# ScalarE's two passes over a slot change places, and the weights get a semaphore of their own

## The reference, cut to what matters

```python
h = _L0_tok_ref(x, ...)
h = h + _L0_attn_ref(_layernorm(h, axis=-1), ...)
h = h + _L0_ffn_ref(_layernorm(h, axis=-1), ...)
```

```python
scores, idx = jax.lax.top_k(sim, PK_TOPK)
final_scores, pk_idx = jax.lax.top_k(score, FINAL_TOPK)
final_scores = jax.nn.softmax(final_scores, axis=-1)
k = jnp.einsum('bnhk,bnhkd->bnhd', kv_scores, keys_table[ind])
v = jnp.einsum('bnhk,bnhkd->bnhd', kv_scores, values_table[ind])
```

## Time and profile before

| | before |
|---|---|
| median of 3 runs | 11975.05 us (11971.79 to 11983.34) |
| the profiled execution's own time | 11981.82 us |
| its span, first to last instruction | 11980.0 us |
| PE busy | 11034.8 us (92%) |
| DVE busy | 10219.1 us (85%) |
| POOL busy | 8419.7 us (70%) |
| ACT busy | 7851.7 us (66%) |
| mean granted clock of TensorE | 0.981 |

### The profile page before, as it was taken

The page is one execution under the profiler, slowest core; times in us unless marked ns, Lnnn a source line. Parts: engine busy times, 40 slices in busy tenths (PEclk is TensorE's granted clock), DMA queues, the critical chain, the costliest instruction groups (busy, mean ns, idle before and its releaser), DMA issues.

```text
span 11980.0 us, 263894 instructions
## 1 busy us (share of the span) xinstructions
PE 11034.8 (92%) x70396; PEld 9154.4 (76%) x70396; DVE 10219.1 (85%) x42192; ACT 7851.7 (66%) x17926; POOL 8419.7 (70%) x8196
## 2 busy tenths in 40 slices
PE   3999999999999999999999999999999999999999
PEld 2777777777777777777777777777777777777777
DVE  6889888888888898888888988888889888888883
ACT  2666666666666666666666666666666666666665
POOL 0677777677777777777777777767777777777776
PEclk6999999999999999999999999999999999999999
DMA  2566566565565665665655656656556566566554
GB/s 66 155 173 179 156 174 171 160 175 167 166 177 159 171 179 157 171 172 161 175 166 164 177 158 170 179 155 174 170 161 177 165 168 177 158 172 177 158 170 137
DMA packets 1651836, 1975.58 MB, mean 165 GB/s; under 512 B 336238, under 2 KB 1125870, under 8 KB 1649902
## 3 DMA queue, kind: packets, MB, share of 16 engines
q1 hardware_dynamic: 1387950, 1418.48, 40.8%
q0 software_dynamic: 262144, 537.40, 17.2%
HBM read 1881.20 MB, written 73.40 MB: 163 GB/s over the span
## 4 chain that ended last, share of the span: by engine, by line
PE 57%; DVE 19%; ACT 8%; issue 7%; DMA 6%; SPq 2%; POOL 0%; DVEq 0%; ACTq 0%; POOLq 0%
PE bank L1008 16%; PE bank L1044 10%; PE bank L1031 6%; PE bank L1018 5%; DVE decay L1579 4%; PE bank L891 4%; ACT bank L1255 4%; DMA moving<-keyspace 3%; DVE apart L1709 3%; DMA wide<-states 3%; DVE onehot L1804 2%; PE bank L995 2%; PE bank L972 2%; DVE decay L1588 2%; PE bank L1060 2%
## 5 line engine op out<-in xcount | busy, mean ns | idle before, releaser
L819 POOL DMA_INDIRECT gath<-in_table_dram,rowsT x8192 | 8419.5, 1028 | 3533.0 <-issue 2449.9
L1262 ACT ACTIVATE weight<-bank 128x512 f32<-128x512 f32 x4096 | 2441.0, 596 | 2895.2 <-PE bank L1018 2863.6
L1008 PE MATMUL bank<-weight,rowtab 128*128 128x256 f32 x16384 | 4263.0, 382 | 0.0
L1008 PEld LDWEIGHTS bank<-weight,rowtab 128*128 128x128 f32 x16384 | 3122.9, 191 | 756.2 <-issue 20.6
L1255 ACT ACTIVATE bank<-bank,seventeen 128x512 f32<-128x512 f32 x4096 | 2711.5, 662 | 14.7 <-PE bank L1018 11.5
L1044 PEld LDWEIGHTS bank<-spread,gath 128*128 128x128 f32 x16384 | 2160.3, 192 | 149.6 <-issue 14.5
L1044 PE MATMUL bank<-spread,gath 128*128 128x96 f32 x16384 | 2116.5, 272 | 5.5 <-DMA gath<-in_table_dram,rowsT 5.1
L1031 PE MATMUL bank<-moving,pick_b 96*128 96x512 bf16 x4096 | 1584.5, 387 | 485.1 <-ACT bank L1255 392.4
L1018 PE MATMUL bank<-moving,pick_b 96*128 96x512 bf16 x4096 | 1562.2, 381 | 81.3 <-DMA moving<-keyspace 80.7
L1579 DVE TENSOR_TENSOR_SCAN decay<-decay,wide 128x256 f32<-128x256 f32 x2048 | 1238.4, 670 | 3.3
L1031 PEld LDWEIGHTS bank<-moving,pick_b 96*128 96x128 bf16 x4096 | 438.1, 107 | 924.6 <-ACT bank L1255 738.3
(11 more groups left out here) (268 smaller groups left out, 16949.8 us busy)
## 6 DMA issues: line engine op xcount, KB each, us to landing
rowtab<-in_tableD_dram SPq DMA_DIRECT2D x2048, 256.0 KB
wide<-states SPq DMA_DIRECT2D x512, 512.0 KB
moving<-keyspace SPq DMA_DIRECT2D x4096, 64.0 KB
gath<-in_table_dram,rowsT POOLq DMA_INDIRECT x8192
moving<-keyspace SPq DMA_DIRECT2D x4096, 32.0 KB
pix<-in_x_dram SPq DMA_DIRECT2D x504, 256.0 KB
keyspace<-split SPq DMA_DIRECT2D x256, 256.0 KB
out_dram<-acc SPq DMA_DIRECT2D x64, 64.0 KB
```

Of the source, the lines that this page charges most:

```text
L819: pool.indirect_dma_start(out=gath[:, u % RING, j, :], out_offset=None, in_=table, in_offset=bass.IndirectOffsetOnAxis(ap=rowsT[k][:, col: ...
L1008: mm(dense_ps[:, 0:TOK], rowtab[:, r, s % 2 * 2 + half, :], weight[s % 2][:, half * TOK:(half + 1) * TOK], start=(s % 16 == 0 and half == ...
L1262: ins = af(weight[s % 2][:], zd_ps[s % 2][:], ACT.Exp, scale=-1.0)
```

## The change

ACT does l(n) ahead of w(n-1) in every row of its table. Items that stood between the two stand behind both now; the order of all other items is kept. Every w signals a new semaphore, `weight_ready`; before, w signalled nothing but in the last slot of all. PE's `o` and `d` wait for `weight_ready` where they waited for `over_ready`; `z` still waits for `over_ready`. PE's own order stays.

```diff
-2 w1+0 S.hi3+0 l2+0 F.g+1 F.sq0+2
+2 l2+0 w1+0 S.hi3+0 F.g+1 F.sq0+2
...
-8 w7+0 F.kv2+2 l8+0
+8 l8+0 w7+0 F.kv2+2
...
-24 w23+0 F.sc+2 l24+0
+24 l24+0 w23+0 F.sc+2
...
+        weight_ready = sem("weight_ready")
...
-                    pe.wait_ge(over_ready, b * SLOTS + s + 2)
+                    pe.wait_ge(weight_ready, b * SLOTS + s + 1)
...
-                wait(pe, over_ready, b * SLOTS + s)
+                wait(pe, weight_ready, b * SLOTS + s - 1)
...
-                    pe.wait_ge(over_ready, IMAGES * SLOTS + (0 if s == 0 else 1))
+                    pe.wait_ge(weight_ready, IMAGES * SLOTS - (1 if s == 0 else 0))
...
-                ins = af(weight[s % 2][:], zd_ps[s % 2][:], ACT.Exp, scale=-1.0)
-                if isinstance(b, int) and b == IMAGES - 1 and s == SLOTS - 1:
-                    ins.then_inc(over_ready, 1)
+                af(weight[s % 2][:], zd_ps[s % 2][:], ACT.Exp, scale=-1.0).then_inc(weight_ready, 1)
```

More of the change, by code:

```diff
@@ L143 @@
 ACT_ORDER = """
-0 w63-1 l0+0 k3-1 a5.5-1 F.sq2+2 F.sq3+2 S.E2+0
-1 w0+0 l1+0 K3-1
-2 w1+0 S.hi3+0 l2+0 F.g+1 F.sq0+2
[L147 to L151, removed]
-8 w7+0 F.kv2+2 l8+0
[L153 to L167, removed]
-24 w23+0 F.sc+2 l24+0
[L169 to L207, removed]
+0 l0+0 w63-1 k3-1 a5.5-1 F.sq2+2 F.sq3+2 S.E2+0
+1 l1+0 w0+0 K3-1
+2 l2+0 w1+0 S.hi3+0 F.g+1 F.sq0+2
+3 l3+0 w2+0 a6.0-1
+4 l4+0 w3+0 F.sq1+2
+5 l5+0 w4+0 S.n+1 S.mi3+0
+6 l6+0 w5+0 a6.4-1 F.kv0+2
+7 l7+0 w6+0 S.E3+0 F.kv1+2 a6.5-1
+8 l8+0 w7+0 F.kv2+2
+9 l9+0 w8+0 F.kv3+2 S.tb+1 S.s0+1
+10 l10+0 w9+0 F.kv4+2 F.kv5+2
+11 l11+0 w10+0 F.kv6+2 F.kv7+2 S.s1+1 a7.0-1
+12 l12+0 w11+0
+13 l13+0 w12+0 F.kv8+2 S.s2+1 F.kv9+2
@@ new lines @@
+14 l14+0 w13+0
+15 l15+0 w14+0 a7.4-1 F.kv10+2 F.kv11+2
+16 l16+0 w15+0 a7.5-1 F.rs0+2 k0+0
+17 l17+0 w16+0 K0+0
+18 l18+0 w17+0 F.t0+2 S.s3+1 a0.0+0
+19 l19+0 w18+0
+20 l20+0 w19+0
+21 l21+0 w20+0 a0.4+0
+22 l22+0 w21+0
+23 l23+0 w22+0
+24 l24+0 w23+0 F.sc+2
+25 l25+0 w24+0 a0.5+0
+26 l26+0 w25+0
+27 l27+0 w26+0 a1.0+0
+28 l28+0 w27+0
+29 l29+0 w28+0 F.t1+2
+30 l30+0 w29+0 a1.4+0
+31 l31+0 w30+0 F.rs1+2
+32 l32+0 w31+0 k1+0 a1.5+0 K1+0
+33 l33+0 w32+0 S.wd+1
+34 l34+0 w33+0 F.t2+2 S.ln+1 F.ez+2
@@ new lines @@
+35 l35+0 w34+0 S.hi0+1 a2.0+0
+36 l36+0 w35+0 F.sg+2
+37 l37+0 w36+0
+38 l38+0 w37+0 S.mi0+1 S.hi1+1 a2.4+0
+39 l39+0 w38+0 S.cp+1 F.dt0+2
+40 l40+0 w39+0 F.xd+2 F.dt1+2
+41 l41+0 w40+0 a2.5+0 F.dc0+2
+42 l42+0 w41+0 S.E0+1 S.mi1+1
+43 l43+0 w42+0 a3.0+0
+44 l44+0 w43+0 F.dc1+2
+45 l45+0 w44+0 F.dc2+2
+46 l46+0 w45+0 a3.4+0
+47 l47+0 w46+0 F.dc3+2
+48 l48+0 w47+0 k2+0 F.dc4+2 a3.5+0 K2+0
+49 l49+0 w48+0
+50 l50+0 w49+0 F.dc5+2 S.E1+1
+51 l51+0 w50+0 a4.0+0
+52 l52+0 w51+0 S.wg+1
+53 l53+0 w52+0 F.dc6+2
@@ L208 @@
+54 l54+0 w53+0 F.dc7+2
+55 l55+0 w54+0 a4.4+0
+56 l56+0 w55+0 a4.5+0
+57 l57+0 w56+0
+58 l58+0 w57+0 S.hi2+1
+59 l59+0 w58+0 a5.0+0
+60 l60+0 w59+0
+61 l61+0 w60+0
+62 l62+0 w61+0 a5.4+0
+63 l63+0 w62+0 S.mi2+1
 """
```

## The result

The changed kernel takes **12014.01 us** (median of 6 runs, 12000.78 to 12027.21) against 11974.92 (6 runs, 11970.24 to 11983.34) for the kernel before on the same chip. The ratio is **1.0034 [1.0024, 1.0044]**: 0.34% slower, some 41 us. The forecast was 3 us faster. The time lies in its range, and it is that of its second rival (12011 to 12038).

What follows compares the result with a forecast made beforehand. Bound by a PE chain through l in a period's first half, then DVE with transfers or a mixture in alternate periods. 2 x 0.34 - 0.57 = 0.11 us per pair, some 31 pairs: 3 us off 11975, 11972; range 11905 to 12035.

Steps and rivals of the forecast that it cites:

- second rival: Items held back on ACT reach PE late in rows 8, 15, 55: 36 or 63 us slower, 12011 to 12038; chance 0.21.
- The count of a slot: Bare slots on PE: z starts 0.50 us earlier, but next o waits for w, at 1.69 instead of 1.90; gain 0.21.
- The four items without cover: ACT items made 0.57 later in rows 8, 15, 25, 55 cost PE 0.43, 0.57, 0.12 and 0.57 us.
- z's waits: PE's idle time ahead of z for l would shrink from 392 us to under 100.
- DVE's idle time ahead of acc: DVE's waits ahead of L1838 would hardly change.
- what DVE lets through in the first half: Up to row 39, DVE's nearly gapless stretch passes on only 0.34 us a period of PE's gain.
- every gap as used to the full: DVE's idle gaps of 0.15, 0.47 and 0.21 us after 4928.91 turn 0.49 late into 0.34 early by row 39.
- lies beside DVE's work: Row 55's 0.57 us loss is hidden in one of two periods and on the path in the other.
- if row 55 turned up in the chain of every period: Sign that the prediction is wrong: row 55 in the chain that ended last in all periods.
- earlier z changes nothing: Second half of the period whose chain is DVE's own with transfers: no gain there, the first half's is carried on.
- The likeliest case: Two periods gain 2 x 0.34 and lose 0.57 in row 55, 0.11 net: 3 us faster, 11972 us.
- The prediction's 1.99 from PE alone: PE's gains up to row 38 before losses: seven bare rows at 0.21 and row 24's 0.52, 1.99 us a period.

Runs made afterwards that it cites:

- e5: Kernel before with its ACT table unchanged, only every w signalling and PE's o and d waiting for that signal: 11986.91 us, ratio 1.0007.
- the swap: Changed kernel, but l and w only exchange places and all items between them stay between: 11900.92 us, 0.9939 of the kernel before.
- e11: The swap, but in rows 2, 25 and 34 S.hi3, a0.5 and F.t2 stand behind both passes: 11934.8 us, 0.9961 of the kernel before.
- e1: Changed kernel with the new order in rows 0 to 38 alone, rows 39 to 63 as before: 12012.31 us, 1.0026 of the kernel before.
- e9: The swap, but F.sc of row 24 stands behind w as in the changed kernel: 11916.51 us, 0.9940 of the kernel before.
- e6: Changed kernel with the new order in rows 39 to 63 alone, and row 55's a4.4 between l and w: 11976.83 us, 0.9992 of before.
- e8: The swap, but row 55's a4.4 stands behind both passes: 11950.93 us, 0.9967 of the kernel before.
- e10: The swap, but row 55's a4.4 stands ahead of both passes: 11876.28 us, 0.9912 of the kernel before.
- e12: The swap, but one item in each of rows 2, 8, 15, 25, 34, 41 and 55 stands ahead of both passes: 11851.27 us, 0.9889 of before.

## Why the prediction was wrong

**Right.** The count of a slot: the wait goes from z to the next o and only part of it is gained (0.17 to 0.18 for 0.21). w's semaphore costs nothing (e5). The four items without cover, and nearly their sizes: row 8 grew by 0.54 (0.43 forecast), row 15 by 0.51 (0.57), row 25 by 0.15 (0.12), row 55 by 0.68 (0.57). z's waits fell to 49.9 us (under 100 forecast), `a.5` waits twice in a period, 127 times, and DVE's idle time ahead of acc hardly changed (815.0 us, 806.0 before). The table has twenty-one items between w and l, not twenty; nothing hangs on it.

**Wrong, first: what DVE lets through in the first half ("0.34 us").** The step counted "every gap as used to the full": 0.15, 0.47 and 0.21. The first went, as it was said. The other two did not: 0.47 ahead of h is still 0.47, and 0.21 ahead of the split is 0.26 in the mean. DVE in the changed kernel:

```profile
5144.72 0.47 DVE L1837 SCALAR_TENSOR_TENSOR acc<-bank,rrow,acc 128x64 f32<-128x64 f32 x2
...
5154.79 0.29 DVE L1533 TENSOR_TENSOR h<-bank,rf 128x128 f32<-128x128 f32 x1 [0.47 <-PE bank L914]
```

and PE beside it:

```profile
5145.34 0.67 PE L1061 MATMUL bank<-xT,wq_ffn 128*128 128x256 f32 x2
...
5154.20 0.56 PE L914 MATMUL bank<-proj,turned 65*128 65x64 f32 x4
```

PE's L1061 in row 26 starts 0.15 after DVE's acc has ended, 5144.72+0.47 = 5145.19. From there PE's instructions follow one another without a gap, and DVE's with gaps of a few hundredths: PE reaches L914 8.86 later, and h follows it. DVE waits for PE, and PE had waited for DVE's acc. So this gap stayed with every table that was tried; in the swap (total us, times, longest):

```profile
DVE h L1533 <- PE bank L914: 31.3, 63, 2.4
...
DVE split L1783 <- ACT split L1246: 1.0, 2, 0.9
```

The third gap is another matter. It is gone in the swap, and it is back in e11 with `a0.5` and `F.t2` late: with these late ACT is late for the split too. Which of the two does it was not tried. In the changed kernel rows 25, 26 and 34 grew by 0.15+0.30+0.38, and row 24's 0.47 went into that. Of the forecast 0.83 from three gaps the wall became 0.22 shorter (43.56 to 43.34).

Against it stands the early loss. By o19 PE is behind by the two rows' 1.05 and 0.09 of row 10, less the 0.50 of three bare slots: 0.64, where 0.43 was forecast. With 0.22 given back that is 0.42 a period, 27 us, and the first half measured 31 us slower (e1) instead of 22 faster. Rows 0 to 2 are left out of this count. Together they changed by +0.17 in the changed kernel, by -0.14 in e1, with the same order in these rows, and by +0.25 in the swap, so nothing is to be read from them.

One item was left out altogether: row 34's `F.t2` was not among "four are not covered". With row 25's and row 2's it costs 26 us (e11); how much each has was not tried, but row 2 shows no loss there. And `F.sc`, to which the step gave DVE's whole lateness, costs nothing that can be measured (e9).

**Wrong, second: row 55 "lies beside DVE's work" in one of two periods.** It was read from one window of the chain that ended last, 4973:5053, where that period's second half ran through DVE. The same view over row 55 of all periods would have told otherwise. In the kernel before, the transposes of row 55 stand in the chain in 56 of 64 periods, and that window fell on one of the eight others. The chain in row 55 two periods earlier:

```profile
4654.13 0.35 ACT prob L1293 x2
4654.48 0.47 ACT prob L1294 x2
...
4654.99 0.55 PE bank L1073 x3
```

The prediction named the sign by which it would be wrong ("if row 55 turned up in the chain of every period"), and in the changed kernel that is 60 of 64. By e6, e8 and e10 a pass of ACT ahead of `a4.4` is worth about 34 us (30 with the clock taken off), some 0.5 a period, in both kinds. The prediction had 31 x 0.57 = 18. The chain of the changed kernel also shows what joins row 55 to DVE:

```profile
5222.59 0.55 PE bank L1074 x3
...
5226.38 0.23 PE bank L1019
...
5226.63 0.58 SPq L744
...
5230.34 7.62 DMA wide<-states
...
5237.98 1.30 DVE decay L1587 x2
```

PE's o of row 57 frees SyncE to issue the keys (L744), more issues follow in SyncE's order, the transfer of the states is among them, and DVE waits for it. So it goes in 42 of 63 periods. Even the full count of one chain isn't the price: in the swap row 55 is in the chain in 33 of 64 periods, and one pass more ahead of it still cost 34 us within 22 (e8), with row 55 in the chain in 59.

**Wrong, third: "earlier z changes nothing" in the second half.** Rows 43, 46, 52, 54 and 56 get shorter as well, by 0.13 to 0.21. It is probably why the second half alone lost 25 us and not 34. The run that comes nearest to showing it by itself is e6: without row 55's loss the second half gives 10 us, within 11. The same error made the step too small where nothing is held back: the swap gains 73 us, 1.1 a period, and by the table 0.48 of it in the wall and 0.70 outside. The prediction's 1.99 from PE alone would have been 127 us.

**Put together.** The likeliest case had 0.68 of gain and 0.57 of loss in two periods. With the measured prices: the swap gives 1.14 a period (73/64); rows 8 and 15 take 0.94, row 55 0.52, rows 2, 25 and 34 0.41, and 0.73 of loss a period is left; the changed kernel's 41 us are 0.64. The second rival's mechanism came true and its time too, but it counted no loss in row 34 and no gain in the second half; that its sum fits is in part chance.

## What to carry to other kernels

When two instructions of an in-order engine change places, write the items between them down as items of the change: each that ends up behind both is later by one of them, and its price is what its waiter has of cover. The exchange alone was worth 0.6% here, and with the same items behind instead of between it became a loss of 0.3%; with those that have no cover ahead of both it is 1.1%. A gap on the next engine is slack only if what ends it does not itself wait for that engine: follow it back once around before counting it. Count in how many periods an item is in the chain before taking one period for the rule. And an item that is off the chain may be off it by very little; move it by one place both ways, and the two prices tell.

## What the runs showed of the hardware

A signal on each of 4096 ACTIVATEs costs nothing that can be measured here: 1.0007 [0.9998, 1.0015] (e5). In a bare slot the next o comes 0.04 later than the durations added up to (1.73 for 1.69), and it is two terms that were off. ACT's first pass starts 0.41 after o where l stands first, and 0.47 where w did. The hand-over from the end of w to the next o takes 0.14, not the 0.05 that passes from the end of l to z; these are the medians of rows 6, 14, 22, 30, 38 and 46 over 56 periods, the same in all six. What makes these hand-overs differ was not tried.

Among the runs of one kernel the device time and the mean granted clock move against each other, by some 7 us for 0.001 (0.981 to 0.984 is the spread of the profiled executions). In the traces, away from the span's two ends, the lower of the clock's two levels comes in stretches of 3.4 or 6.8 us: 53 of them in the kernel before, 52 in the changed one and 38 in e12.
